# A decoder's last stage on Trainium2: the coupling's twist moved from TensorE to GpSimd, its cycles cut into groups of two batches, and the last output product reordered by head pairs

## The reference, cut to what matters

```python
x5 = _layernorm(x4 + _L1_xattn_ref(ctx, x4, ...))   # 16 heads of 64, output projection Wout
# last sublayer, input x = x5
gf = _global_net(x.mean(axis=1, keepdims=True), ...)        # per batch: gelu, gelu, sigmoid
out = x
for _ in range(3):                                          # NUM_CYCLES
    tf = _coupling_net(out, ...)                            # per token: 3 x gelu(h @ w + b), sigmoid
    combined = 0.7 * gf + 0.3 * tf
    coupling = 0.1 + adaptive_range * (combined - 0.5) * 2.0
    out = out + coupling * _twist(out)                      # twist: [p_r, -p_i, -o_r, o_i] of 4 parts of 32
out = _layernorm(x + out)
```

## Time and profile before

| | us |
|---|---|
| median of 3 runs | 1072.19 (1072.03 to 1072.51) |
| the profiled execution, its own time | 1068.93 |
| its span (first to last instruction) | 1067.2 |
| TensorE busy, share of the span | 986.8 (92%) |
| VectorE busy | 723.6 (68%) |
| ScalarE busy | 702.7 (66%) |
| GpSimd busy | 571.7 (54%) |

### The profile page before, as it was taken

How to read it: one execution, slowest core, us unless ns; L and a number is a source line. 1 busy time by engine, 2 the same in 40 slices (tenths; PEclk the granted TensorE clock), 3 DMA queues, 4 the chain that set the end, 5 groups by cost and what they waited for, 6 DMA issues and landing times.

```text
span 1067.2 us, 16268 instructions
## 1 busy us (share of the span) xinstructions
PE 986.8 (92%) x5218; PEld 778.3 (73%) x5218; DVE 723.6 (68%) x1589; ACT 702.7 (66%) x1397; POOL 571.7 (54%) x437
## 2 busy tenths in 40 slices
PE   6959889999999579999999999999999999998895
PEld 3737678888888357787878878888788888786432
DVE  6886886556556768887885777757676757761247
ACT  4336654342333437988886888868988868887453
POOL 8110330028437317778785877757777757776001
PEclk9989999999999669999999999999999999999998
DMA  7100000000000032222231223213132313210001
GB/s 246 8 1 2 1 2 1 2 1 1 1 2 24 16 86 69 60 63 66 60 71 44 68 61 74 56 43 85 44 86 52 77 43 73 56 43 1 1 1 40
DMA packets 46399, 46.14 MB, mean 43 GB/s; under 512 B 23095, under 2 KB 29163, under 8 KB 45803
## 3 DMA queue, kind: packets, MB, share of 16 engines
q1 hardware_dynamic: 46315, 45.10, 17.6%
HBM read 7.60 MB, written 1.05 MB: 8 GB/s over the span
## 4 chain that ended last, share of the span: by engine, by line
PE 82%; DVE 9%; ACT 5%; issue 2%; POOL 1%; DMA 0%; POOLq 0%; DVEq 0%; ACTq 0%
PE PS L1595 79%; PE PS L1607 2%; DVE X_ODD L1110 1%; DVE BIG L1193 1%; DVE mx L1190 1%; DVE st L1092 1%; ACT BIG L790 1%; ACT BIG L1041 1%; DVE X_EVEN L1110 1%; ACT BIG L820 1%; POOL rs L653 1%; ACT PHI L1042 1%; DVE VLO L1414 0%; ACT BIG L798 0%; DVE QA L1405 0%
## 5 line engine op out<-in xcount | busy, mean ns | idle before, releaser
L748 POOL TENSOR_TENSOR PLO<-BIG,PHI 128x512 fp32r<-128x512 f32 (+1 forms) x320 | 413.4, 1292 | 170.5 <-ACT PHI L1042 156.6
L1041 ACT ACTIVATE BIG<-PS 128x512 f32<-128x512 f32 (+1 forms) x320 | 192.2, 601 | 84.5 <-PE PS L1595 79.3
L1456 DVE TENSOR_REDUCE mxm<-PS 128x1 f32<-128x512 f32 x256 | 174.1, 688 | 54.5 <-PE PS L1595 51.0
L1042 ACT ACTIVATE PHI<-PS 128x512 fp32r<-128x512 f32 (+1 forms) x320 | 191.3, 598 | 0.0
L653 POOL TENSOR_TENSOR rs<-ve,half_neg 128x4 f32<-128x4 f32 (+1 forms) x29 | 29.9, 1032 | 210.0 <-DVE ve L1100 209.3
L1595 PE MATMUL PS<-KA,QA 128*128 128x512 f32 (+1 forms) x512 | 137.2, 333 | 4.1 <-DVE mxm L1456 2.3
L1595 PE MATMUL PS<-PHI,VLO 128*128 128x512 f32 (+1 forms) x320 | 131.3, 410 | 0.0
L1595 PE MATMUL PS<-QA,KA 128*128 128x512 f32 (+1 forms) x320 | 129.3, 404 | 0.9 <-issue 0.5
L1595 PE MATMUL PS<-PLO,VHI 128*128 128x512 f32 (+1 forms) x320 | 126.4, 395 | 1.0 <-POOL PLO L748 1.0
L1595 PE MATMUL PS<-PHI,VHI 128*128 128x512 f32 (+1 forms) x320 | 125.9, 394 | 0.0
L1595 PE MATMUL PS<-QB,KB 128*128 128x512 f32 (+1 forms) x320 | 125.7, 393 | 0.0
(11 more groups left out here) (264 smaller groups left out, 1962.6 us busy)
## 6 DMA issues: line engine op xcount, KB each, us to landing
KA<-TK SPq DMA_DIRECT2D x128, 128.0 KB, 2.4
QA<-TQ SPq DMA_DIRECT2D x64, 128.0 KB, 2.3
QB<-TQ SPq DMA_DIRECT2D x64, 128.0 KB, 2.3
KA<-TK SPq DMA_DIRECT2D x128, 19.5 KB, 1.8
X_EVEN<-in_x SPq DMA_DIRECT2D x4, 256.0 KB, 3.4
VXA<-in_L_ffn_Wg SPq DMA_DIRECT2D x1, 1024.0 KB, 5.7
VXA<-in_L_ffn_Wu SPq DMA_DIRECT2D x1, 1024.0 KB, 7.6
VXA<-in_L_ffn_Wd SPq DMA_DIRECT2D x1, 1024.0 KB, 9.1
```

The costliest lines, as they stand in the source:

```text
L748: pool.tensor_tensor(PLO[0:rows, g % 4, :], PX[0:rows, g % 4, :], PHI[0:rows, g % 4, :].bitcast(F32), ALU.subtract).then_inc(rest_pool, 1)
L1041: act.activation(PX[0:rows, g % 4, :], PS[0:rows, g % 2, :], ACT.Exp, scale=SCALE_W)
L1042: act.activation(PHI[0:rows, g % 4, :], PS[0:rows, g % 2, :], ACT.Exp, scale=SCALE_W).then_inc(lead_ready, 1)
L1456: dve.tensor_reduce(mxm[:, p % 2, h, m:m + 1], PS[:, 2 + g % 2, :], AX.X, ALU.max).then_inc(mu_free, 1)
```

## The change

1. `coupling_groups` gives two groups of two batches in every cycle. In cycle 0 the global net's layers stand in the second group; so does the transposed input of batch 3, as before ahead of its first layer.
2. The twist matmuls go, with the matrix and their lane V tasks. GpSimd copies the halves of the state instead, each 64x512, into SH (`turn_halves`): the second copy waits for the first, and the turn of a batch for its state of the cycle before (in cycle 0: for its transposed input). All turns stand in GpSimd's queue behind the power of batch 3's normalisation, ahead of the four last powers. The signs are a column `sign`, multiplied into cA and cB on VectorE. VectorE's product reads SH, in SBUF, in place of the bank.
3. The output product of batches runs over head pairs outside and token blocks inside. It waits for all quotients but those of the last pair, and before that pair's four matmuls for these. The one of batch 3 stands ahead of the three transposed inputs.

```diff
 def coupling_groups(c):
-    return [range(B)] if c < CYCLES - 1 else [range(2), range(2, B)]
+    return [range(2), range(2, B)]
...
-                if c == 0 and layer < 3:
+                if c == 0 and group[0] and layer < 3:
                     t += [("gn", layer)]
...
-            t += [("twist", c, b)]
...
+        SH = REG[:, 4096:6144].rearrange("p (b n) -> p b n", b=B)
...
-        N_CONST = 20
+        N_CONST = 18
...
-            pool.memset(twist[:], 0.0).then_inc(consts, 1)
+            pool.memset(sign[:], 1.0).then_inc(consts, 1)
...
-            for n, (fill, off) in enumerate(((1.0, -64), (-1.0, -64), (-1.0, 64), (1.0, 64))):
-                cols = twist[:, 32 * n:32 * n + 32]
-                pool.affine_select(out=cols, in_=cols, compare_op=ALU.not_equal, fill=fill, base=off - 32 * n,
-                                   pattern=[[-1, 32]], channel_multiplier=1).then_inc(consts, 1)
+            for n, lo in enumerate((32, 64)):
+                pool.wait_ge(consts, 16 + n)
+                pool.memset(sign[lo:lo + 32, :], -1.0).then_inc(consts, 1)
+            pool.wait_ge(consts, 18)
             pool.memset(VBD[:], 0.0).then_inc(vbd_zero, 1)
...
             last_layers()
             rstd(("E", B - 1))
+            def turn_halves(c, b):
+                if c:
+                    pool.wait_ge(state_ready, B * (c - 1) + b + 1)
+                else:
+                    pool.wait_ge(a_free, LA["xT", "F", b] + 1)
+                n = 2 * (B * c + b)
+                pool.wait_ge(rstd_ready, LN["E", B - 1] + 1)
+                if n:
+                    pool.wait_ge(turned_ready, n)
+                pool.tensor_copy(SH[0:DW, b, :], FS[DW:P, b, :]).then_inc(turned_ready, 1)
+                pool.wait_ge(turned_ready, n + 1)
+                pool.tensor_copy(SH[DW:P, b, :], FS[0:DW, b, :]).then_inc(turned_ready, 1)
+            for c in range(CYCLES):
+                for b in range(B):
+                    turn_halves(c, b)
+            pool.wait_ge(turned_ready, 2 * B * CYCLES)
             for b in range(B):
                 rstd(("F", b))
...
-            dve.tensor_scalar_mul(cA[:], ar1[:], 0.3)
+            dve.tensor_scalar(cA[:], ar1[:], sign[:], 0.3, ALU.mult, ALU.mult)
...
             link(dve.tensor_scalar_add(cB[:], cB[:], 0.1))
+            link(dve.tensor_scalar_mul(cB[:], cB[:], sign[:]))
...
-                    n = LV["twist", c, b]
-                    dve.wait_ge(v_full, n + 1)
-                    dve.tensor_tensor(CP[:, b, :], CP[:, b, :], bank_v(n), ALU.mult).then_inc(v_free, 1)
-                    dve.wait_ge(v_free, n + 1)
+                    dve.wait_ge(turned_ready, 2 * (B * c + b + 1))
+                    link(dve.tensor_tensor(CP[:, b, :], CP[:, b, :], SH[:, b, :], ALU.mult))
                     dve.tensor_tensor(FS[:, b, :], FS[:, b, :], CP[:, b, :], ALU.add).then_inc(state_ready, 1)
...
-                    pe.wait_ge(on_ready, 2 * NHP * (b + 1))
-                    for t in range(NT):
-                        for c in range(NHP):
-                            ins = mm(bank[:, P * t:P * t + P], OT[:, c, P * t:P * t + P], wout1s[:, c, :], start=c == 0, stop=c == NHP - 1)
+                    pe.wait_ge(on_ready, 2 * NHP * (b + 1) - 2)
+                    for c in range(NHP):
+                        if c == NHP - 1:
+                            pe.wait_ge(on_ready, 2 * NHP * (b + 1))
+                        for t in range(NT):
+                            ins = mm(bank[:, P * t:P * t + P], OT[:, c, P * t:P * t + P], wout1s[:, c, :],
+                                     start=c == 0 and t == 0, stop=c == NHP - 1, skip_group_check=True)
...
-            pe.wait_ge(on_ready, 2 * PAIRS)
+            task(EPILOGUE[0])
             for b in range(B - 1):
                 input_f(b)
-            task(EPILOGUE[0])
...
                     lane_a(("cn", c, layer, b), lambda bank: mm(bank, w[:], src[:, b, :]))
-                    if layer == 3:
-                        lane_v(("twist", c, b), lambda bank: mm(bank, twist[:], FS[:, b, :]))
-                if c == 0 and layer < 3:
+                if c == 0 and group[0] and layer < 3:
```

More of the change, by code:

```diff
@@ L335, in decoder @@
         iota = sb("iota", [P, E])
-        twist = sb("twist", [P, P])
+        sign = sb("sign", [P, 1])
         ctx_sb = sb("ctx_sb", [CK, B, D])
@@ L489, in decoder @@
         q_in, k_in, kt_in = ([sem(f"{n}{r}") for r in range(3)] for n in ("q_in", "k_in", "kt_in"))
-        gs_ready, coef_ready, state_ready, out_sem = (sem(n) for n in ("gs_ready", "coef_ready", "state_ready", "out_sem"))
+        gs_ready, coef_ready, turned_ready, state_ready, out_sem = (sem(n) for n in ("gs_ready", "coef_ready", "turned_ready", "state_ready", "out_sem"))
         block = es.enter_context(nc.Block())
```

## The result

The changed kernel takes 1062.99 us (median of 4 runs, 1061.06 to 1064.03), the kernel before in the same series 1072.11 (1070.03 to 1072.51). The ratio is 0.992, with a 95% interval of 0.9908 to 0.9932: 7.3 to 9.9 us faster. The forecast was 1065.2, 7.0 faster, in a range of 1062.9 to 1068.6. The profiled execution took 1061.06, its span is 1058.9; against the profiled one of before the span is 8.3 shorter.

What follows compares the result with a forecast made beforehand. TensorE was taken as the bound, mostly in the untouched wide loop; behind it a pause, slow clock, TensorE-ScalarE alternation, then VectorE. Steps along the path gained 7.0 off the 1072.19 median: 1065.2 us, range 1062.9 to 1068.6.

Steps and rivals of the forecast that it cites:

- first gelu: ScalarE's first gelu after the output product and input transposes: expected at 992.0, 2.7 us earlier than before.
- coda: Stretch from the wide loop's last product to the span's end; 87.0 us in the kernel before.
- Output product: Batch 3's product after the wide loop: starts at 980.2 without pause, full clock, VectorE gets its sum 4.9 us earlier.
- Cycle 0 and the new wait: Two groups, global tanh ending at 1008.75; all coupling needs that tanh, so TensorE waits twice at cycle 1's start.
- the slot of the global product: Global matmul's place in the ring of banks in cycle 0's second group, costing each layer 0.85 us.
- GpSimd's copies: Turning state halves by 64x512 copies: 0.62 us each, about 1.3 per turn, hidden behind 3.9 us of coupling work.
- The slope of the selections: Basis for the copy's cost: 128x16 and 128x128 selections differ by 94 ns for 112 elements, giving 620 ns.
- the two-input subtraction: Upper bound for a copy's cost: GpSimd's 128x512 two-input subtraction, 1293 ns.
- The hold: VectorE's product and sum in batch 1's first coupling each wait for a GpSimd copy: 2 x (0.62 - 0.14) = 0.96 us.
- Cycles and tail: Cycles 1 and 2 without twists: last cycle's coupling 6.6 us earlier; VectorE bounds the tail, saving 0.38, total gain 7.0.
- The clock rival: Clock falls to 1.2 GHz in cycle 1's new waits, losing 1.5 to 2 us: 1067.0; chance 0.18.
- The other rivals: No hold (1064.2, chance 0.12), 1.29 us copies (1067.2, 0.09), product not early (1068.8, 0.04), GpSimd copies as chain (1079.7, 0.04).

Runs made afterwards that it cites:

- ahead_whole: Kernel before, with batch 3's output product moved whole ahead of the three transposed inputs, still waiting for all quotients; ratio 1.000 to the kernel before.
- early_global: Changed kernel with the global net's layers and batch 3's input moved earlier in cycle 0; 1059.58 us, ratio 0.9879 to the kernel before.
- turn_later: Changed kernel with each GpSimd turn also waiting for the next batch's state; ratio 0.9912 to the kernel before.
- t_only: Kernel before with only the twist moved to GpSimd's copies, groups and output product as before; ratio 1.0034 to the kernel before.
- tg: Changed kernel with the output product put back as before, so twist on GpSimd and two groups only; ratio 0.9960 to the kernel before.
- pt: Changed kernel without the two groups in cycles 0 and 1; ratio 0.9957 to the kernel before.
- tg_fill: Kernel tg with one matmul of constants ahead of each of TensorE's two waits at cycle 1's start; ratio 0.9956 to the kernel before.
- g_only: Kernel before with only two groups in every cycle, twist on TensorE and product as before; ratio 1.0010 to the kernel before.
- copies_twice: Changed kernel with each of GpSimd's 24 copies made twice; ratio 0.9915 to the kernel before.

## Why the prediction was right

The forecast's steps, in us behind the loop's last product, against the changed kernel's profile:

```
step                                       forecast   measured
VectorE takes the product's sum               7.4        7.19
first gelu                                   11.8       11.38
global tanh ends                             28.6       28.13
batch 1's matmul of cycle 1                  34.1       33.43
first coupling of the last cycle             56.6       56.01
from there to the end                        23.5       23.2
coda                                         80.0       79.2
```

The median of 1062.99 lies 2.2 below the forecast and only 0.1 inside the range. The coda explains 0.8 of that. The rest (0.5 ahead of the coda, 0.9 between the profiled executions and the medians) is none of the forecast's steps, so that the number stayed inside the range is in part luck.

**Output product.** Right in mechanism: it fills the pause and keeps the clock at 1.00. It brings the first gelu 3.2 earlier, forecast 2.7. ahead_whole shows that the order by head pairs, which lets it start before the last quotients, is what makes it work.

**Cycle 0 and the new wait.** Right: two pauses at the start of cycle 1, both released by the state's sum. early_global shows that the wait is for the global tanh. First gelu to the end of that tanh took 16.75, as forecast; the slot of the global product should have been 4.81 - 3.92 = 0.89 there, not 0.85, which would have moved it by 0.1.

**GpSimd's copies.** 0.61 for one, forecast 0.62. The slope of the selections was the right ruler, the two-input subtraction was not. The 0.77 of the Trainium skill's GPSIMD Engine Reference, which I had given beside it, is not what this copy takes.

**The hold.** Right in mechanism (turn_later), mis-sized: forecast 2 x 0.48, measured 2 x 0.29. What the path got back without it was 0.57 (turn_later). I took the copy's whole 0.62 less the product's 0.14 of start-up. But the copy is issued during the scaling and runs its own start-up then: 0.44 of it is left when the product is issued (1011.50 - 1011.06), and 0.43 of the second copy when the sum is. The Trainium skill's SBUF — State Buffer (Who interferes with whom) says that the later one blocks until the other's instruction is over; the ends of the rows above agree. One hold I didn't see: the one of batch 3's normalisation (2.26 instead of 1.11 from 990.26). In the changed kernel its result is first needed at 998.73, so it costs nothing; in t_only it cost 1.15.

**Cycles and tail.** VectorE became the bound of the tail, as forecast; the sum of steps was 0.8 too long: 0.4 ahead of the first gelu, 0.4 for the hold, 0.3 in the tail, less some 0.2 that the cycles took more than I had.

**The clock rival.** It had 0.18. It didn't occur in the profiled execution of the changed kernel, but it did in tg, t_only and pt, and cost 1.7 in tg, as I had put it (1.5 to 2). The changed kernel's four executions span 3 us; whether such falls make that spread wasn't shown, only the profiled one can be looked into. The two faster ones (1061.06 and 1062.48) had a mean granted clock of 0.973, the two slower 0.970 and 0.969, but a part of such differences arises ahead of the coda: the loop's end lies up to 2.1 us apart in kernels that are the same until there. The other rivals did not come: holds are there, the product starts at once, the copies take less than 1.29.

What I did not see in the forecast is how the parts depend on each other. I had it as a sum of steps along one path; each step held only because the others were there.

## What to carry to other kernels

Work taken off the bounding engine pays only if something else covers the wait that this work was covering. Here the twist matmuls covered the coupling: without them alone the kernel got slower (1.0034, of which a held normalisation and a fallen clock are the greater part by my estimate), without them and with two groups that alternate it gets 3 to 4 us faster. Look first for the pauses of TensorE near the change: filling one pays twice, its own length and the slower clock behind it. And before moving work to GpSimd, write down which VectorE operations will run beside it, those with two SBUF inputs, the scalings and the normalisation here, and which of them is on the path.

## What the runs showed of the hardware that I had not expected

The same two pauses (0.88 and 1.36 us) left the granted clock at 1.00 in the changed kernel and at 0.50 for 3.4 us in tg; a pause of 0.83 with small ones behind it brought 0.50 in tg_fill and not in tg. At the pause of 2.1 us behind the loop the slow stretch lasted 3.4 us in the kernel before, where it began 1.7 us behind the loop's last product, and 6.8 us in ahead_whole and g_only, where it began after 0.4 us. So codas of the same code can lie 1 to 2 us apart, and a single profile of a change that adds pauses can miss their price.

VectorE's scaling of one SBUF tensor also waits for a GpSimd copy (0.97 instead of 0.54 in copies_twice), while the copies in turn wait for it (0.87 instead of 0.61). So does the normalisation, four 128x128 operations: 2.26 to 2.27 in all kernels with turns (2.79 in copies_twice), 1.11 to 1.12 in all without. In the changed kernel neither comes second on the path.
